# Paged attention block on one core: the SyncE loop folded from two groups to one, and the first mixing stage turned within its own product

## The reference

```python
x = x + einsum('bct,bcd->bdt', x, W0[cond])                  # mixes the 32 tokens of a sequence
x = x + x @ base_weight.T + base_bias + (x @ A[id].T) @ B[id].T   # base product and the sequence's adapter, rank 16
q, k, v = x @ Wq.T, x @ Wk.T, x @ Wv.T                       # 32 query heads, 8 key/value heads of 128
q, k = rope(rmsnorm(q)), rope(rmsnorm(k))
x = x + softmax(q [k_cache[pages], k].T / sqrt(128) + mask) [v_cache[pages], v] @ Wo.T
x = x + einsum('bct,bcd->bdt', x, W3[cond])
```

## Time and profile before

| | us |
|---|---|
| median of three runs | 2315.6 |
| the profiled execution: its time | 2315.53 |
| its span, first to last instruction | 2313.8 |
| PE busy | 2251.0 (97%) |
| DVE busy | 1765.2 (76%) |
| ACT busy | 1594.6 (69%) |

### The profile page before, as it was taken

The page is one execution under the profiler, slowest core; times in us unless marked ns, Lnnn a source line. Parts: engine busy times, 40 slices in busy tenths (PEclk is TensorE's granted clock), DMA queues, the critical chain, the costliest instruction groups (busy, mean ns, idle before and its releaser), DMA issues.

```text
span 2313.8 us, 56498 instructions
## 1 busy us (share of the span) xinstructions
PE 2251.0 (97%) x15392; PEld 2008.7 (87%) x15392; DVE 1765.2 (76%) x5613; ACT 1594.6 (69%) x4413; POOL 557.0 (24%) x712
## 2 busy tenths in 40 slices
PE   8999999999999899999999999999999999999999
PEld 5778888888887899989989989989999989997777
DVE  3434777777777999889989989989989989995332
ACT  4423666666666988878878878878878878884221
POOL 1002444444443221221221222122122212210000
PEclk9999999999999999999999999999999999999999
DMA  5335333333327777777777777777777778765332
GB/s 169 95 97 172 105 102 101 100 101 103 116 82 236 245 260 265 258 238 259 257 235 257 256 243 249 259 254 248 254 252 257 250 238 263 245 227 182 135 122 97
DMA packets 347991, 456.02 MB, mean 197 GB/s; under 512 B 34538, under 2 KB 280874, under 8 KB 343726
## 3 DMA queue, kind: packets, MB, share of 16 engines
q1 hardware_dynamic: 308430, 315.83, 42.8%
q0 software_dynamic: 36864, 134.23, 16.6%
q10 hardware_dynamic: 2528, 4.29, 0.5%
HBM read 374.53 MB, written 79.69 MB: 196 GB/s over the span
## 4 chain that ended last, share of the span: by engine, by line
PE 80%; SPq 6%; issue 6%; DMA 3%; DVE 3%; ACT 2%; ACTq 0%; POOL 0%; DVEq 0%; POOLq 0%
PE oP L1289 14%; PE S L1256 13%; PE S L1213 11%; PE oP L1213 11%; PE S L1307 8%; PE bank L1137 8%; PE bank L1320 6%; SPq L379 3%; PE oP L1137 3%; PE oP L1167 2%; DMA regK<-kT_cache 2%; SPq L377 2%; PE oP L1299 1%; DVE k_lo L1002 1%; PE oP L1159 1%
## 5 line engine op out<-in xcount | busy, mean ns | idle before, releaser
L1289 PEld LDWEIGHTS oP<-regC,regK 128*128 128x128 f32 x4096 | 534.4, 193 | 36.9 <-issue 5.0
L1289 PE MATMUL oP<-regC,regK 128*128 128x128 f32 x4096 | 544.8, 276 | 1.3
L730 ACT CAST k_hi<-regK 128x544 fp32r<-128x544 f32 x512 | 331.5, 647 | 160.6 <-PE S L1256 127.4
L1017 DVE CUSTOM_DVE_ANT_0 regC<-S,mask 128x544 f32<-128x544 f32 x512 | 368.7, 720 | 66.5 <-issue 58.9
L1002 DVE TENSOR_TENSOR k_lo<-regK,k_hi 128x544 fp32r<-128x544 f32 x512 | 368.3, 719 | 35.3 <-ACT k_hi L730 35.0
L744 ACT ACTIVATE regC<-regC,nmx 128x544 f32<-128x544 f32 x512 | 387.9, 758 | 1.9 <-DVE nmx L1017 1.8
L1137 PE MATMUL bank<-ident,regC 128*128 128x128 f32 x2048 | 311.0, 275 | 24.5 <-ACT regC L790 24.5
L571 POOL TENSOR_TENSOR regC<-regC 128x256 f32<-128x256 f32 x320 | 245.6, 788 | 278.6 <-DVE regC L977 278.6
L790 ACT COPY regC<-bank 128x512 f32<-128x512 f32 x512 | 298.8, 584 | 5.5 <-PE bank L1137 5.5
L550 POOL COPY idx<-idx_all 128x4 int32 (+1 forms) x65 | 30.4, 470 | 1071.0 <-PE oP L1299 969.8
L553 POOL DMA_INDIRECT regK<-v_cache,idx x256 | 266.9, 1043 | 79.3 <-issue 79.1
(11 more groups left out here) (136 smaller groups left out, 4319.5 us busy)
## 6 DMA issues: line engine op xcount, KB each, us to landing
regK<-kT_cache SPq DMA_DIRECT2D x1024, 128.0 KB
qkT_d<-regC SPq DMA_DIRECT2D x160, 256.0 KB, 2.3
regC<-qkT_d SPq DMA_DIRECT2D x64, 512.0 KB, 8.0
oT_d<-regC SPq DMA_DIRECT2D x64, 256.0 KB, 6.3
regK<-oT_d SPq DMA_DIRECT2D x16, 1024.0 KB, 5.4
regC<-wqk SPq DMA_DIRECT2D x10, 1024.0 KB, 5.3
v_d<-regC SPq DMA_DIRECT2D x32, 256.0 KB, 2.3
regK<-qkT_d SPq DMA_DIRECT2D x64, 128.0 KB
```

Source lines behind the costliest of these rows:

```text
L730: nc.scalar.copy(k_hi[u % 2].rearrange("p (s t) -> p s t", t=PSIZE), k_sb[b][:, :, h, :]).then_inc(s_khi, 1)
L1017: nc.vector.tensor_tensor_reduce(out=p_sb[u % 4], in0=scores, in1=mask[:], scale=-SCALE, scalar=3e38, op0=ALU.add, op1=ALU.min, accum_out= ...
L1289: last = nc.tensor.matmul(oP[:, at:at + P], v_sb[b][:, m, h * D:(h + 1) * D], pT_sb[u % 2][:, m * P:(m + 1) * P], start=(h < 4 and m == 0) ...
```

## The change

- SP's loop of the attention stage holds one group instead of two and makes 14 passes instead of seven.
- `btab` has one half. The next group's table is loaded at the fourth sequence of a group, not the first, and a new wait (`s_tabin`) stands ahead of the first sequence of the next group.
- First stage: the 32x32 identity (`eye`) is added to `w0` and the 128x128 identity to the diagonal of the base weight, once, on DVE. So `x1` needs no adding: `mixed` takes `x_sb` as the weights and `bd0` as the moving side and gives the mixed tile already turned, in four products of 128 columns. `mix0`, `turn1` and `add0` go, and `add1` becomes a copy. `mixed` runs one tile ahead of `base`, into two banks by turns.
- In the last round `add1` stands ahead of `split_w` on DVE.
- SP loads `wb` second, after the first `x` tile; `load_x` waits for `s_tx1` (mixed and turned) in place of `s_x1`.

```diff
@@ sync engine, start @@
-            for j in range(2):
-                load_x(0, j)
+            load_x(0, 0)
             sp.dma_start(wb_sb, wb.rearrange("p c n -> p (c n)")).then_inc(s_wb, 16)
+            load_x(0, 1)
@@ sync engine, attention @@
-            def group(g, par, first, last):
+            def group(g, first, last):
                 for k in range(BT):
                     b = g * BT + (k + 2)
                     if not (last and k >= 2):
+                        if k == 0:
+                            ge(sp, s_tabin, g * 16)
                         sp.wait_ge(s_qp, g * (2 * BT) + 2 * (k + 1))
                         load_q(b, k % 2)
                         sp.wait_ge(s_klo, g * UG + HK * (k + 1))
                         load_own_k(b, k % 2)
-                        load_pages(btab[0:1, par, k * NPP:(k + 1) * NPP], k % 2)
+                        load_pages(btab[0:1, k * NPP:(k + 1) * NPP], k % 2)
                         sp.wait_ge(s_po, g * BT + (k + 1))
                         load_own_v(b, k % 2)
-                    if k == 0 and not last:
-                        load_table(g + 1, 1 - par, BT * NPP)
+                    if k == 3 and not last:
+                        load_table(g + 1)
-            group(0, 0, True, False)
-            with sp.Fori(0, NT // 2 - 1) as gg:
-                group(gg * 2 + 1, 1, False, False)
-                group(gg * 2 + 2, 0, False, False)
-            group(NT - 1, 1, False, True)
+            group(0, True, False)
+            with sp.Fori(1, NT - 1) as g:
+                group(g, False, False)
+            group(NT - 1, False, True)
@@ vector engine @@
-                nc.vector.tensor_tensor(x2_sb[j], bank[2 + j % 2], x1_sb[j], ALU.add).then_inc(s_x2, 1)
+                nc.vector.tensor_copy(x2_sb[j], bank[2 + j % 2]).then_inc(s_x2, 1)
+            dve.wait_ge(s_const, 48)
+            dve.wait_ge(s_w0, 16)
+            nc.vector.tensor_tensor(w0_sb, w0_sb, eye.unsqueeze(1).to_broadcast([P, CONDS, C]), ALU.add).then_inc(s_w0i, 1)
+            dve.wait_ge(s_wb, 16)
+            for c in range(HC):
+                at = slice(c * T + c * P, c * T + (c + 1) * P)
+                nc.vector.tensor_tensor(wb_sb[:, at], wb_sb[:, at], ident[:], ALU.add).then_inc(s_wbi, 1)
@@ tensor engine @@
-                nc.tensor.matmul(bank[j % 2], bd0[j], x_sb[j], start=True, stop=True).then_inc(s_mm0, 1)
-            def turn1(i, j):
-                transposes(bank[4], x1_sb[j]).then_inc(s_tx1, 1)
+                ge(pe, s_x1T, t - 1)
+                for c in range(HC):
+                    at = slice(c * P, (c + 1) * P)
+                    last = nc.tensor.matmul(bank[4 * (j % 2)][:, at], x_sb[j][:, at], bd0[j], start=True, stop=True)
+                last.then_inc(s_tx1, 1)
```

More of the change, by code:

```diff
@@ L286, in build @@
         s_bd3 = [sem(f"s_bd3{i}") for i in range(2)]
-        s_w3 = sem("s_w3")
+        s_w3, s_tabin = sem("s_w3"), sem("s_tabin")
         s_l3, s_out, s_outst = sem("s_l3"), sem("s_out"), sem("s_outst")
@@ L368, in _, with load_table @@
                 sp.dma_start(w_raw[j], wqk[j].rearrange("p c n -> p (c n)")).then_inc(s_w, 16)
-            def load_table(g, par, count):
-                sp.dma_start(btab[0:1, par, 0:count],
-                             bt_row[0:1, bass.ds(g * (BT * NPP) + 2 * NPP, count)]).then_inc(s_x2yst, 16)
+            def load_table(g):
+                sp.dma_start(btab[:], bt_row[0:1, bass.ds(g * (BT * NPP) + 2 * NPP, BT * NPP)]).then_inc(s_tabin, 16)
             def load_pages(table, par, first=0, count=NPP):
@@ L445, in group @@
                         load_own_k(b, k % 2)
-                        load_pages(btab[0:1, par, k * NPP:(k + 1) * NPP], k % 2)
+                        load_pages(btab[0:1, k * NPP:(k + 1) * NPP], k % 2)
                         sp.wait_ge(s_po, g * BT + (k + 1))
                         load_own_v(b, k % 2)
-                    if k == 0 and not last:
-                        load_table(g + 1, 1 - par, BT * NPP)
[L451 to L454, removed]
+                    if k == 3 and not last:
+                        load_table(g + 1)
+                    if k == 1 and not first:
+                        ge(sp, s_x2yst, g * 16 - 16)
                         sp.dma_start(x2r, x2_d[bass.ds(g - 1, 1)].rearrange("a p n -> p (a n)")).then_inc(s_x2r, 16)
@@ L620, in x1_turned @@
                 act.wait_ge(s_tx1, t + 1)
-                nc.scalar.copy(x1T_sb[j], bank[4]).then_inc(s_x1T, 1)
+                nc.scalar.copy(x1T_sb[j], bank[4 * (j % 2)]).then_inc(s_x1T, 1)
                 act.wait_ge(s_x1T, t + 1)
@@ L654, in round1a @@
                             split_w(j // 2, j // 2, j % 2 * 2 + c)
-            for dst, src in ((ident[:], ident_c), (hmask, hmask_c)):
+            for dst, src in ((eye, eye_c), (ident[:], ident_c), (hmask, hmask_c)):
                 act.dma_start(dst, src).then_inc(s_const, 16)
@@ L905, in round1a @@
                 for j in range(4):
-                    if not (last and j >= 2):
-                        add0(i, j + 2)
                     own_rank(i, j)
@@ L912, in round1a @@
                         x2_low(i, j - 1)
+                    add1(i, j)
                     if last:
@@ L1138, in transposes, with mixed @@
                 return last
-            def mix0(i, j):
+            def mixed(i, j):
                 i, j, t = tile(i, j)
@@ L1184, in round1a @@
                 for j in range(4):
-                    if not (last and j >= 2):
-                        mix0(i, j + 2)
                     if not (last and j == 3):
-                        turn1(i, j + 1)
+                        mixed(i, j + 1)
                     if first and j == 0:
@@ L1197, in _ @@
             pe.wait_ge(s_ones, 4)
[L1198 to L1201, removed]
+            mixed(0, 0)
+            pe.wait_ge(s_const, 48)
             round1a(0, True, False)
@@ L1427 @@
         "ident_c": np.eye(P, dtype=np.float32),
+        "eye_c": np.tile(np.eye(C, dtype=np.float32), (BT, 1)),
         "iota_c": np.tile(np.arange(L, dtype=np.float32), (P, 1)),
```

34 lines of the change are left out of this document (11 added, 23 removed).

## The result

The changed kernel takes 2350.05 us (four runs, 2338.95 to 2350.67), against 2314.89 us (2313.25 to 2317.2) for the kernel before on the same chip: ratio 1.0148, 95% interval 1.013 to 1.0166, so 35 us slower. The forecast was 2355.

The account below looks back on a forecast made before the run. PE, busy 97% of the span, was taken as the bound. 2315.5 us plus 42 for SP's seven more returns and −2.7 for the first stage gave 2355 us, range 2344 to 2365, widened to 2342 to 2371.

Parts of the forecast that it names:

- The price of one return: SP's attention loop: each return costs 6.0 us (5.0 to 7.0); seven more returns, +42 us (35 to 49).
- The page table's wait: New `s_tabin` wait on SP before the next group's queries: 0, upper end 1 us for each of 14 groups.
- `mixed` at 1.02 us: First stage, PE's step: 14 `mixed` at 1.02 us (other end 0.89) replace `mix0` and `turn1`, −3.1 us (−4.9).
- The start: First stage's start: first base product +0.1 us, PE's half-speed clock +1.5 us; ends 0 and +3.
- The end of the stage: First stage's end: two splits moved behind the last `add1` lie beside PE's work, −1.2 us.
- The projections: Stage between the first stage and attention: predicted difference 0.
- Rival 1: SP's smaller loop body stays resident, all return misses go: 2277 to 2300 us, say 2283; chance 8%.
- Rivals 2 and 3: SP's miss only 3.3 us: 2297 us, chance 5%; table's wait longer than the stall: 2369 to 2383 us, chance 9%.
- Rival 4: SP's longer stall costs PE nothing in either kernel, only the first stage shows: 2313 us; chance 1%.

Follow-up runs that it names:

- slim_dve_padded: Changed kernel without page-number bounds checks in SP's group loop, eight memsets moving DVE's attention loop back to its old place: 2270.42 us, 0.9812 of the kernel before.
- dve_padded: Changed kernel plus eight small DVE memsets putting DVE's attention loop back where it began before: 2425.12 and 2426.47 us, 1.0029 and 1.0032 of the kernel before, slow chips.
- after_again: The changed kernel itself, unaltered, measured again in a later set: 2337.87 us, 1.0102 of the kernel before (2312.34 us).
- unrolled_dve_padded: Changed kernel with SP's 14 attention passes written out and eight memsets restoring DVE's loop place: 2345.84 us, 0.9704 of the kernel before, slow chip.
- slim_misaligned_dve_padded: `slim_dve_padded` with checks kept for the very first sequence ahead of SP's loop, moving the 301-instruction loop 32 on: 2271.12 us, 0.9816 of the kernel before.

## Why the prediction was right, and where its terms were off

Half of the mechanism was right: SP returns 13 times instead of six, each return waits for code, the gap has the length it had before, every group becomes long, and the attention stage grows by 40.4 us (predicted +42). The other half, that each of these gaps reaches PE as the six had, is not what the trace shows. The total is close by luck: part of it comes from a miss on DVE that the forecast did not have, and errors of opposite sign met.

- *The price of one return, 6.0 us.* 12 windows of the changed kernel are 1057.7 us, against 12 × 82.87 = 994.4 without a return; the stretch from 1959.7 us to the last score product, which holds the thirteenth return, is 166.1 us, against 158.8 in `slim_dve_padded`. Together 70.6 us in 13 groups, 5.4 each, where the six of the kernel before were 6.0 each (1030.4 − 994.4 = 36.0). Thus +34.6, not +42. But these are not SP's alone. Of PE's idle time in the 13 groups 34.0 us are its waits for DVE behind DVE's misses, and 16.2 us the waits for late pages, where the six returns before had 24.5. In its own terms the forecast's seven more returns added nothing to the wait that it followed; DVE's loop, whose place it took as given, added 34 us of another.
- *What that leaves open.* The two overlap: while PE waits for DVE, SP's pages gain that time. Thirteen returns at the 4.1 us of PE's idle time that each had before would be 53 us, an estimate, against the 50.2 measured for both together, so with DVE's loop in place SP's gaps alone might have cost as much. `dve_padded` would tell on the fast chip, and it was run only on the slow ones.
- *The price is no property of the gap.* With 6 us of gap and 110 us of spare time it goes with long groups; with the same gap and 267 us it is nothing; on the slow chips a group with a return is 1 to 2 us longer. ACT waits for pages in ten places (32.1 us, 890 to 2100 us), where 13 or so were forecast. That all the gaps would reach PE was taken from the earlier trace rows, which hold for SP as busy as it was, and for a DVE that returned freely.
- *The same kernel again* (`after_again`) was 25.5 us slower than the kernel before, just under the lower end of the forecast's range (2342, or 26.5 us). Its groups are 87.4 us on average. PE's idle time divides the same way, 32.9 us behind DVE's misses and 15.3 for pages.
- *The page table's wait, 0.* Right for the 13 returns: one wait of 2.8 us in all. Missed is the first group. SP enters the loop there without a return, so nothing covers the table: 821.12 us issued, 825.9 there, 3.9 us of waiting, and +6.0 us from the first score product to PE's first return (+1.8 in `after_again`, 179.2 us). The prediction had said that the wait would be bare without the stall and didn't look for the pass that has none.
- *`mixed` at 1.02 us.* It took 0.89, the other end. From the second base product to the last, 14 steps took 85.4 us (27.38 to 112.82), 6.1 each, where they took 89.7 (26.19 to 115.90), 6.4 each: −4.3, predicted −3.1.
- *The start.* First adapter product at 17.90 for 18.09, −0.2 (+0.1 predicted); the first step from base to base 7.5 us for 6.2, +1.3 (clock, +1.5 predicted): the twelve products took 4.73 us, where the later ones take 2.95, after PE had waited 5.6 us for `wb_lo`.
- *The end of the stage*, last base product to first projection: 3.1 us for 4.8, −1.7 (−1.2 predicted).
- *The projections*, −1.9 us: scatter. In all versions of the kernel they took 599.6 to 602.3 us, with no order in it.
- *Rival 1*, that the smaller body stays, falls for 429 instructions, and its condition was put too simply. It is reached at 301 in one place and not 32 instructions on. (By its own terms the rival's upper end is 2305 us, not 2300.)
- *The rule of the Trainium skill*, page "Runtime: NRT & Kernel Launch", section "Instruction fetch mechanics", has 512 instructions outside PE, in two blocks of 256. The traces don't agree: the packets hold 128, and two blocks of 256 that let SP's 301 return freely in one place and not 32 on would let its 429 return freely too, since that loop begins 128 instructions behind the first; it missed 13 of 13 times.
- *Rivals 2 and 3* fall: the gaps are 5.2 to 6.4 us, and SP's waits hardly name the table. *Rival 4*, that the returns cost PE nothing, is true for a kernel whose SP has 16 us more per group; here late pages hold PE up in seven of the 13 groups.

Open, besides the share of DVE and SP in the 35 us: why the changed kernel took 2350 us in one comparison and 2338 in the other (one of the four runs of the first was 2338.95 as well), and what makes the attention stage longer on two of the chips.

On the fast chip `slim_dve_padded` and its two variants beat both kernels, at 0.9812 [0.9794, 0.9831] of the kernel before: SP has time to spare, and the attention windows are PE's own 82.9 us.

## What to carry to other kernels

A loop on an engine that issues transfers has two prices that a diff doesn't show: the gap at each return, if the body doesn't stay loaded, and how much spare time that engine has to make it up. Read both (the branch's gap, the engine's own waits) before counting returns. Here a cheaper body made the gaps free: with 13 of them or none the slim kernel took the same time. A gap counts only where PE waits for what stands behind it, so look at the place of PE's idle time in the group and not only at its sum. Any edit on an engine, even of instructions far ahead, moves the loops behind it, so look at the first record behind every loop's branch, on the engines too that the change was not about.

## What the runs showed of the hardware

- A code packet of SP, ACT or DVE here is 8.2 KB (202 packets, 1.65 MB) and 128 instructions (34 packets for 4263 records of SP in `unrolled_dve_padded`). All the loops of this study agree with one rule: one that touches three such blocks returns in 0.2 to 0.3 us (DVE's 308 in the place before, ACT's 260, SP's 301 and 304), one that touches four or more misses at each return (DVE's 308 moved by 8, SP's 301 moved by 32, SP's 429 and 852, and the 402 and 399 of the projections). The block's edges are worked out for each engine from which of its loops miss, not measured by themselves.
- A miss brings about five packets for a loop that touches four blocks (`slim_misaligned_dve_padded` 137 packets, `slim_dve_padded` 72, for 13 misses of SP; the changed kernel 202, `dve_padded` 139, for 13 of DVE).
- A miss leaves DVE idle for 2 to 3 us in its attention loop, in the same stage in which SP's gap is 4.1 to 6.8. What makes SP's longer was not tried.
- SP's bounds check of a register is two instructions and about 0.25 us; 16 of them take 4 us, more than the read of the 16 numbers (median 1.0 us).
